# Weight block sums taken from fewer early tiles, Wo's second sums one group later, another final output taken ahead, and butterfly sums made by accumulating DMAs

## Chip, cores and metric

One core of one Trainium2 chip (trn2). The metric is device microseconds of one execution of the whole program. The engines are TensorE (PE in the profile; PEld is its weight load), VectorE (DVE), ScalarE (ACT), GpSimd (POOL) and SyncE (SP); SP, ACT and POOL issue the DMAs.

## What is computed

Eight chunks of 512 tokens with 512 features are normalised, go through a linear attention and through a gated feed-forward part whose weights are meant in a Walsh-Hadamard basis, and the product of both is added to the input:

```
xn = layernorm(x)
k, v, q = xn @ W{k,v,q}.T + b                      # elu(k)+1, elu(q)+1
context = phi_q * cumsum(phi_k * v) * SCALE
s = context @ Wo.T + bo
y = fwht(xn * SU_ug) / 64
h = silu(y @ W_gate.T * ws_gate) * (y @ W_up.T * ws_up)
g = silu(fwht(h * SU_dp) / 64 @ W_down.T * ws_down)
out = x + s * g
```

D is 512, the hidden size of the feed-forward part 2048. The transforms are taken on the weights, once, and not on the tokens.

## The kernel before

**Precision and products.** Each f32 operand is split in a high and a low f16 part, and a product takes three f16 matmuls of 128x512 per pair of operands. Chunks are worked in four pairs. Pair 0 uses plain 2x2 block products, 12 matmuls for a tile. Pairs 1 to 3 use Winograd's form of Strassen's algorithm: seven products (P1 to P7) for four blocks, whose left factors are, besides three plain blocks, four block sums S1 to S4 of the weights, and whose right factors are sums T1 to T4 of the tokens.

**Pieces and groups.** The weights of K, V, Q (two pieces each), of gate and up (eight each, alternating) and of Wo (two, numbers 22 and 23) make 24 pieces, and a group `g` is the work with piece `g`. In pair 0, tile `4 * g + j` is the j-th output block of group `g`; it is also the clock of the preparatory work, which `first_weights` (DVE) and `first_group` (ACT) hang behind certain tiles.

**Butterflies.** Gate's and up's weights of a block `i` (0 to 7) arrive as one load into `raw_ug`. `fly_rows(i, level)` on DVE makes two levels of sums and differences over four rows: level 0 adds and subtracts neighbours from `raw` into `mid`, level 1 from `mid` back into `raw`; each is one addition and one subtraction of 128x1024 f32. `mid` is `fly` (in `x_res`) for `i >= 2`. Level 1 counts `flown` up. ACT and DVE then split the result, PE folds the last levels in, and the piece is stored to DRAM (`scr_g`) and, unsplit, to `scr_f`. `fly_down_level` and `take_down` do the like for the down weights, for which PE's `fold_down` waits.

**Block sums.** For each piece `n` a pass runs over four engines: POOL loads the raw piece (`load_blocks`, for Wo `load_o_blocks`), DVE makes S1 to S4 (`s_sums`, four instructions of 128x256), ACT writes the high half (`s_high`), DVE the low half (`s_low`), POOL stores (`store_sums`). A pass's load waits for the sums of the pass before, its `s_high` for the store before. `S_TILES` lists the tiles of pair 0 behind which DVE makes the sums of passes 0, 1, ...; the next `S_RING - S_EARLY` passes are written out by hand in the stretch at the end of pair 0, and the remaining ones (`late_sums`) hang behind groups of pair 1. `S_RING` is 12 before and after. The first five loads of pair 1's pieces wait for the stores of all 12 (`s_stored`).

**Order of the work.** Each engine's program is one fixed list with semaphore waits; nothing is scheduled at run time. POOL's list alternates loads and stores of the passes with loads for statistics (`load_stats`), reductions over partitions and the accumulating DMAs that add x to an output (`add_tokens`). `STATS_AT` names the groups of pair 1 behind which DVE takes statistics of the next pair's chunks.

**The last outputs.** In pair 3 DVE multiplies gate and attention output (`gated`); POOL then adds x by an accumulating DMA and SP stores, except for the last `LAST_BY_DVE` outputs, where x is loaded beforehand (`load_last_res`) and DVE adds it. For the very last, `last_ahead` multiplies and adds what is known, ACT scales the gate (`scaled_gate`), and `last_output` adds the last product straight from its bank. SP stores the eight outputs strictly in order.

Of the kernel before, what the change touches and what calls it, by code (L numbers as in the profile page):

```python
# [109 lines left out]
OUTS_BEHIND = (8, 11)  # L110
LAST_BY_DVE = 3
# [20 lines left out]
STATS_AT, LATER_STATS_AT = (18, 20), (8, 10)  # L132
# [22 lines left out]
EARLY_STORES = (3, 5)  # L155

# [123 lines left out]
def build(nc, x, x_t, wk_t, wv_t, wq_t, wo_t, ug_t, down_t, vecs, ident_in, hada_in, signs_in, out):  # L280
# [7 lines left out]
    with ExitStack() as ctx_stack:  # L288
# [82 lines left out]
        scaled_gate = work[:, 0, :]  # L371
# [51 lines left out]
        s_late_stored = [sem(f"s_late_stored{s}") for s in range(2)]  # L423
        o_stored, s_o_loaded = sem("o_stored"), sem("s_o_loaded")
# [459 lines left out]
        def _(pool):  # L884
# [39 lines left out]

            def add_tokens(p, n):
# [42 lines left out]
            for n in range(KB):  # L968
                down_bound(n)
            for n in range(PIECES):  # L970
# [40 lines left out]
        def _(act):  # L1011
# [327 lines left out]

            def seven_and_o(p):  # L1340
# [16 lines left out]
                if p == PAIRS - 1:  # L1357
                    c, t = tile_at(p, 2 * TB - 1)
                    act.wait_ge(gate_ready, 8 * p + 8)
                    act.wait_ge(out_scaled, p + 1)  # L1360
                    act.activation(scaled_gate, gate_of(c, t), ACT.Copy, scale=o_out[:, 0:1]).then_inc(gate_scaled, 1)
# [67 lines left out]
            s_high(S_EARLY + 1)  # L1429
            silu_outs(0)  # L1430
            take_out(0)
            s_high(S_EARLY + 2)
            x_high(1, 0)
            t_high(1, 0)
            s_high(S_EARLY + 3)
            x_high(1, 1)
            t_high(1, 1)
            s_high(S_EARLY + 4)
# [27 lines left out]
        def _(dve):  # L1466
# [561 lines left out]
            def last_ahead(p):  # L2028

                c, t = tile_at(p, 2 * TB - 1)  # L2030
                dve.wait_ge(copied, 3 * nth(p, GROUPS + 1) + 2)
                dve.wait_ge(gate_ready, 8 * p + 8)
# [4 lines left out]
            def last_output(p):  # L2037

                c, t = tile_at(p, 2 * TB - 1)
# [656 lines left out]
```

## Time and profile before

| | |
|---|---|
| time, median of 3 runs | 1297.45 us (1297.43 to 1297.5) |
| the profiled execution's own time | 1299.55 us |
| span of the profiled execution | 1297.7 us |
| PE busy | 1260.4 us, 97% |
| DVE busy | 940.5 us, 72% |
| ACT busy | 617.0 us, 48% |
| POOL busy | 100.1 us, 8% |
| DMA: moved, mean | 220.97 MB, 170 GB/s |
| granted TensorE clock, mean | 0.998 |

The span is the time from the first to the last event of the core in the profile; the profiled execution took 2.1 us more than the median of the runs. Matmuls are pipelined and overlap, so that a matmul's mean of 379 ns is not the distance of two. Times in the rows below are us from the span's start unless marked ns, and L numbers are lines of the kernel before.

### The profile page before, as it was taken

What the parts mean: (1) busy time and instruction counts of PE and PEld (TensorE: products, weight loads), DVE (VectorE), ACT (ScalarE), POOL (GpSimd) and SP (SyncE); (2) the same over time, 40 slices, a digit from 0 to 9 for tenths busy, and PEclk for the clock granted to TensorE, in tenths of its full rate; (3) what the DMA queues carried; (4) which work ended last, traced back from release to release, by engine and by line L of the source; (5) the groups of instructions that cost most, each with busy time, mean ns of one, the idle gap of its engine ahead of it and who ended that gap; (6) DMA issues with size and microseconds to landing.
All of it is one profiled execution on the core that took longest, in us unless ns stands there. A gap on an engine that the chain in (4) does not pass through costs nothing.

```text
span 1297.7 us, 16157 instructions
## 1 busy us (share of the span) xinstructions
PE 1260.4 (97%) x5896; PEld 569.9 (44%) x5896; DVE 940.5 (72%) x1420; ACT 617.0 (48%) x911; POOL 100.1 (8%) x150
## 2 busy tenths in 40 slices
PE   5999999999999999989999999999999999999997
PEld 3543444444444444434444444444444444444443
DVE  6989999978746777867882778776773767775714
ACT  5894565631335655543343555554233655554212
POOL 1001001111110000210022001000001000000001
PEclk9999999999999999999999999999999999999999
DMA  9533463777765256565377424323526433232424
GB/s 365 225 130 122 170 225 124 260 245 266 230 229 183 106 197 234 219 217 213 136 218 240 158 107 153 125 103 99 204 96 194 146 114 122 106 130 74 130 89 106
DMA packets 62112, 220.97 MB, mean 170 GB/s; under 512 B 7248, under 2 KB 15184, under 8 KB 47440
## 3 DMA queue, kind: packets, MB, share of 16 engines
q1 hardware_dynamic: 41696, 170.37, 36.2%
q0 software_dynamic: 13056, 37.49, 9.9%
q10 hardware_dynamic: 7280, 12.06, 2.6%
q8 instruction: 47, 0.77, 0.2%
q14 instruction: 33, 0.27, 0.1%
HBM read 166.40 MB, written 53.50 MB: 169 GB/s over the span
## 4 chain that ended last, share of the span: by engine, by line
PE 75%; DVE 11%; ACT 5%; issue 5%; DMA 3%; POOL 0%; SPq 0%; DVEq 0%; ACTq 0%
PE bank L2409 39%; PE bank L2595 13%; PE bank L2289 11%; PE bank L2475 7%; PE bank L2500 2%; PE bank L2620 2%; ACT work L1212 1%; ACT work L1215 1%; DMA h_all<-scr_f 1%; DVE work L1653 1%; PE bank L2334 1%; PE bank L2520 1%; DVE work L1637 1%; DVE work L1680 1%; DVE work L1643 1%
## 5 line engine op out<-in xcount | busy, mean ns | idle before, releaser
L2409 PE MATMUL bank<-xops,ring 128*128 128x512 f16 x2772 | 604.8, 380 | 10.2 <-DVE work L1680 5.5
L2409 PEld LDWEIGHTS bank<-xops,ring 128*128 128x128 f16 x2772 | 269.6, 98 | 344.5 <-issue 16.2
L2289 PE MATMUL bank<-xops,ring 128*128 128x512 f16 x1008 | 225.2, 379 | 0.8 <-DVE ring L1809 0.8
L1195 ACT ACTIVATE work<-bank 128x512 f32<-128x512 f32 x198 | 117.7, 595 | 216.7 <-PE bank L2409 202.2
L1637 DVE TENSOR_TENSOR work<-bank,work 128x512 f32<-128x512 f32 x198 | 133.5, 686 | 115.1 <-PE bank L2409 102.8
L2595 PE MATMUL bank<-h_all,ring 128*128 128x512 f16 x768 | 166.7, 379 | 0.2 <-DVE work L1637 0.2
L2289 PEld LDWEIGHTS bank<-xops,ring 128*128 128x128 f16 x1008 | 98.0, 98 | 124.2 <-issue 8.6
L2595 PEld LDWEIGHTS bank<-h_all,ring 128*128 128x128 f16 x768 | 75.1, 98 | 91.0 <-DVE work L1637 0.7
L1242 ACT ACTIVATE h_all<-work 128x512 f16<-128x512 f32 x116 | 70.3, 624 | 63.3 <-DVE work L1680 63.2
L1689 DVE TENSOR_TENSOR h_all<-work,h_all 128x512 f16<-128x512 f32 x116 | 79.3, 686 | 6.1 <-ACT h_all L1242 4.7
L1643 DVE SCALAR_TENSOR_TENSOR work<-work 128x512 f32<-128x512 f32 x64 | 44.1, 689 | 51.0 <-ACT work L1215 50.7
L2475 PE MATMUL bank<-h_all,ring 128*128 128x512 f16 x288 | 63.5, 379 | 0.0
L1225 ACT ACTIVATE work<-bank,gate_out 128x512 f32<-128x512 f32 x56 | 38.0, 682 | 44.2 <-PE bank L2289 39.8
L1225 ACT ACTIVATE work<-work,gate_out 128x512 f32<-128x512 f32 x72 | 50.8, 714 | 11.7 <-DVE work L1637 11.4
L1680 DVE SCALAR_TENSOR_TENSOR work<-bank,up_out,work 128x512 f32<-128x512 f32 x56 | 41.8, 747 | 17.3 <-issue 7.4
L1680 DVE SCALAR_TENSOR_TENSOR work<-work,up_out 128x512 f32<-128x512 f32 x72 | 52.1, 743 | 0.3
L2475 PEld LDWEIGHTS bank<-h_all,ring 128*128 128x128 f16 x288 | 28.1, 98 | 34.0
L2500 PE MATMUL bank<-h_all,ring 128*128 128x512 f16 x192 | 41.9, 379 | 0.3 <-DVE x_res L2053 0.3
L1658 DVE TENSOR_TENSOR_SCAN work<-work 128x512 f32<-128x512 f32 x32 | 39.2, 1224 | 1.1
L2409 PE MATMUL bank<-ctx,ring 128*128 128x512 f16 x144 | 34.1, 379 | 0.0
L1212 ACT ACTIVATE work<-work,vec,i_attn 128x512 f32<-128x512 f32 x36 | 29.1, 807 | 9.5 <-DVE work L1637 9.5
L2053 DVE TENSOR_TENSOR h_all<-bank,h_all 128x512 f32<-128x512 f32 x8 | 5.4, 689 | 33.4 <-PE bank L2475 29.6
(281 smaller groups left out, 1316.9 us busy)
## 6 DMA issues: line engine op xcount, KB each, us to landing
ring<-scr_g SPq DMA_DIRECT2D x72, 1024.0 KB, 4.8
ring<-scr_d SPq DMA_DIRECT2D x15, 1024.0 KB, 5.7
scr_g<-ring SPq DMA_DIRECT2D x22, 512.0 KB, 3.4
h_all<-in_ug_t SPq DMA_DIRECT2D x8, 1024.0 KB, 13.1
ring<-in_down_t SPq DMA_DIRECT2D x6, 1024.0 KB, 6.5
scr_g<-ring POOLq DMA_DIRECT2D x12, 512.0 KB, 5.0
work<-in_x_t SPq DMA_DIRECT2D x6, 1024.0 KB, 7.0
scr_g<-h_all POOLq DMA_DIRECT2D x12, 512.0 KB, 2.9
```

The lines of the kernel that those rows point to most:

```text
L1195: act.activation(tile(g, j), chain_bank(g)[:, :], ACT.Copy).then_inc(copied, 1)
L1225: act.activation(tile(g, j), src, ACT.Silu, scale=gate_out[:, at:at + 1]).then_inc(act_tiles, 1)
L1242: act.activation(h[:, i, TILE_OF[j], HI, :], tile(g, j), ACT.Copy).then_inc(h_hi, 1)
L1637: dve.tensor_tensor(tile(g, j), at[:, :], tile(g, j), ALU.add).then_inc(summed, 1)
L1643: dve.scalar_tensor_tensor(tile(g, j), exp_tile(n), 1.0, tile(g, j), ALU.min, ALU.add) \
L1680: dve.scalar_tensor_tensor(tile(g, j), src, up_out[:, at:at + 1], tile(g - 1, j), ALU.mult, ALU.mult).then_inc(h_made, 1)
L1689: dve.tensor_tensor(at[:, LO, :], tile(g, j), at[:, HI, :], ALU.subtract).then_inc(h_ready, 1)
L2289: mm = pe.matmul(plain_bank(g, j)[:, :], at[:, s, 2 * dh + kk, r, :], xops[:, kk, xs, PLAIN_B[dh][c], :], start=(n == 0), stop=(n == len(t ...
L2409: mm = pe.matmul(to[:, :], weight_of(slot, s, b, kk), at, start=(a == 0 and m in (P1, P2, P5)), stop=(a == 5), skip_group_check=True)
L2475: mm = pe.matmul(to[:, :], down_weight(slot, d, i, s), at, start=(i == 0 and n == 0 and m in (P1, P2, P5)), stop=(i == SEVEN - 1 and n == ...
L2500: mm = pe.matmul(to[:, :], rest_weight(slot, half, d + 2 * r, i, s), h[:, i, 2 * half + c, xs, :], start=(m == R22 and n == 0), stop=(n == ...
L2595: mm = pe.matmul(d_bank(c, t)[:, :], w[:, t, ws, :], at[:, s, :], start=(a == 0 and b == 0 and n == 0), stop=(a == KB - 1 and b == KB - 1 ...
```

## The change

Four edits:

- **Butterflies of blocks 3 to 7** (`ADDED_FROM = 3`): at level 0 DVE makes only the difference. The sum is made by POOL: a plain DMA of the one set of rows from the input in DRAM into `fly`, a wait for it, and an accumulating DMA of the other set on top (`add_rows`). `add_rows(i)` waits for `flown` to reach `i`, and DVE's level 1 waits for `rows_added`. All ten DMAs stand in POOL's list ahead of the load of pass 1.
- **Block sums**: tiles 27 and 43 leave `S_TILES`. Five passes instead of seven are made behind tiles of pair 0, and seven instead of five by hand after them, in a new order; POOL's reciprocal root for pair 1 (`rstd_of`) moves behind the store of pass 6.
- **Wo's second sums** (piece 23) hang behind group 18 of pair 1 instead of 17, and the first statistics behind group 17 instead of 18.
- **Last outputs**: `LAST_BY_DVE` is 4 instead of 3, and output 4 is treated as the last one: ahead as far as it is known, then finished from its bank. Its x is a fourth load by SP; its accumulating DMA is gone.

```
-OUTS_BEHIND = (8, 11)
-LAST_BY_DVE = 3
+OUTS_BEHIND = (7, 11)
+LAST_BY_DVE, LAST_AHEAD = 4, (4, 7)
-S_TILES = (27, 43, 59, 72, 76, 80, 84)
+S_TILES = (59, 72, 76, 80, 84)
-S_RING = S_EARLY + 5
-S_LATE_FROM, S_LATE_O = 6, {16: GROUPS, 17: GROUPS + 1}
+S_RING = S_EARLY + 7
+S_LATE_FROM, S_LATE_O = 6, {16: GROUPS, 18: GROUPS + 1}
-STATS_AT, LATER_STATS_AT = (18, 20), (8, 10)
+STATS_AT, LATER_STATS_AT = (17, 20), (8, 10)
+ADDED_FROM = 3
...
+            def add_rows(i):
+
+                to = fly.rearrange("p m a b n -> p (m a) b n")[:, :, 0, :]
+                src = ug_t[i, :, :, :, :].rearrange("p m (a b) n -> p m (a b) n", b=2)
+                pool.wait_ge(flown, i)
+                pool.dma_start(to, src[:, :, 0, :]).then_inc(rows_added, 16)
+                pool.wait_ge(rows_added, 32 * (i - ADDED_FROM) + 16)
+                pool.dma_start(to, src[:, :, 1, :], accum_op=ALU.add).then_inc(rows_added, 16)
...
+            for i in range(ADDED_FROM, FP):
+                add_rows(i)
             for n in range(PIECES):
...
                     load_stats(1, 1)
+                if n == S_EARLY + 1:
                     rstd_of(1)
...
+                    if i >= ADDED_FROM:
+                        prep.after(dve.tensor_tensor(to_high, low, high, ALU.subtract))
+                        return
+                else:
+                    if i >= ADDED_FROM:
+                        dve.wait_ge(rows_added, 32 * (i - ADDED_FROM + 1))
...
+            def last_output(p, n):
+
+                c, t = tile_at(p, n)
+                at, m = ((right_bank(GROUPS + 1), P2), (left_bank(GROUPS + 1), P3))[LAST_AHEAD.index(n)]
+                to = 3 * nth(p, GROUPS + 1) + (1, 3)[LAST_AHEAD.index(n)]
+                dve.wait_ge(product_done, products_to(p, GROUPS + 1, m))
+                dve.wait_ge(gate_scaled, LAST_AHEAD.index(n) + 1)
+                dve.tensor_tensor(o_of(c, t), at[:, :], scaled_gate(n), ALU.mult).then_inc(summed, 1)
+                dve.wait_ge(summed, to)
                 dve.tensor_tensor(res_of(c, t), res_of(c, t), o_of(c, t), ALU.add).then_inc(out_ready, 1)
```

The instructions move as follows. PE's list is the same in both kernels.

DVE in pair 1, at the end of group 17 and the start of group 18 (`h_all<-h_all,s_attn` is `s_low` of piece 22, the four 128x256 rows are the sums of piece 23, BN_STATS the statistics, `work<-bank,up_out,work` the use of the block that frees a bank). Before:

```order
L1838 SCALAR_TENSOR_TENSOR h_all<-h_all,s_attn 128x1024
L1828 TENSOR_TENSOR h_all<-h_all 128x256
L1829 TENSOR_TENSOR h_all<-h_all 128x256
L1830 TENSOR_TENSOR h_all<-h_all 128x256
L1831 TENSOR_TENSOR h_all<-h_all 128x256
L1680 SCALAR_TENSOR_TENSOR work<-work,up_out 128x512
L1689 TENSOR_TENSOR h_all<-work,h_all 128x512
L1680 SCALAR_TENSOR_TENSOR work<-bank,up_out,work 128x512
```

DVE in pair 1, the same place in the changed kernel:

```order
L1860 SCALAR_TENSOR_TENSOR h_all<-h_all,s_attn 128x1024
L1540 BN_STATS stats<-x_res 128x6 x2
L1540 BN_STATS stats<-gates 128x6 x2
L1702 SCALAR_TENSOR_TENSOR work<-work,up_out 128x512
L1711 TENSOR_TENSOR h_all<-work,h_all 128x512
L1702 SCALAR_TENSOR_TENSOR work<-bank,up_out,work 128x512
```

The sums of piece 23 now come one group later, where the statistics stood.

DVE at the end of pair 0, from the token sums of pair 1's first half on (`work<-work`: T1 to T4; `xops<-work,xops` 128x1024 and 128x512: low halves of the plain blocks; 128x1024 x2: low halves of T1 to T4; `ring<-ring` 128x256: sums of a pass; `ring<-ring` 128x1024: its low half). Before:

```order
L1606 TENSOR_TENSOR work<-work 128x512
L1611 TENSOR_TENSOR xops<-work,xops 128x1024
L1613 TENSOR_TENSOR xops<-work,xops 128x512
L1828 TENSOR_TENSOR ring<-ring 128x256
L1829 TENSOR_TENSOR ring<-ring 128x256
L1830 TENSOR_TENSOR ring<-ring 128x256
L1831 TENSOR_TENSOR ring<-ring 128x256
L1621 TENSOR_TENSOR xops<-work,xops 128x1024 x2
L1841 TENSOR_TENSOR ring<-ring 128x1024
```

DVE at the end of pair 0, the same place in the changed kernel:

```order
L1628 TENSOR_TENSOR work<-work 128x512
L1850 TENSOR_TENSOR ring<-ring 128x256
L1851 TENSOR_TENSOR ring<-ring 128x256
L1852 TENSOR_TENSOR ring<-ring 128x256
L1853 TENSOR_TENSOR ring<-ring 128x256
L1633 TENSOR_TENSOR xops<-work,xops 128x1024
L1635 TENSOR_TENSOR xops<-work,xops 128x512
L1863 TENSOR_TENSOR ring<-ring 128x1024
L1643 TENSOR_TENSOR xops<-work,xops 128x1024 x2
```

A pass's low half now stands ahead of T's low halves, and with it ACT's `s_high`, which waits for a store, stands ahead of ACT's high half of T.

DVE in the last pair, from output 3 to the add of group 23's C22 (`h_all<-bank,o_out,h_all`: an attention output added up; `h_all<-bank,work`: a product from its bank times the scaled gate). Before:

```order
L2018 TENSOR_TENSOR h_all<-h_all 128x512
L1633 SCALAR_TENSOR_TENSOR h_all<-bank,o_out,h_all 128x512
L2018 TENSOR_TENSOR h_all<-h_all 128x512
L2033 TENSOR_TENSOR h_all<-h_all 128x512
L2035 TENSOR_TENSOR h_all<-h_all 128x512
L1633 SCALAR_TENSOR_TENSOR h_all<-bank,o_out,h_all 128x512
```

DVE in the last pair, the same place in the changed kernel:

```order
L2045 TENSOR_TENSOR h_all<-h_all 128x512
L2071 TENSOR_TENSOR h_all<-bank,work 128x512
L2073 TENSOR_TENSOR h_all<-h_all 128x512
L2060 TENSOR_TENSOR h_all<-h_all 128x512
L2062 TENSOR_TENSOR h_all<-h_all 128x512
L1655 SCALAR_TENSOR_TENSOR h_all<-bank,o_out,h_all 128x512
```

The count is the same here; the two instructions that take output 4 ahead stand earlier, between outputs 1 and 2.

## Rows read from the trace of the kernel before

**Rows 1.** The page: busy time of each engine, share of the span, instructions.

```profile
PE 1260.4 (97%) x5896; PEld 569.9 (44%) x5896; DVE 940.5 (72%) x1420; ACT 617.0 (48%) x911; POOL 100.1 (8%) x150
```

**Rows 2.** Waits of PE: engine, line, releaser: us in total, times, longest.

```profile
PE bank L2409 <- DVE work L1680: 5.5, 5, 3.4
```

**Rows 3.** Timeline of PE, pair 0: start us, us, engine, line, form [idle before].

```profile
114.83 2.76 PE L2289 MATMUL bank<-xops,ring 128*128 128x512 f16 x12 [0.37 <-DVE ring L1809]
...
125.79 1.12 PE L2334 MATMUL bank<-ring,hada 128*128 128x512 f32 x2 [1.30 <-DVE xops L1955]
```

**Rows 4.** Timeline of DVE, the same stretch of pair 0.

```profile
110.70 1.22 DVE L1899 TENSOR_TENSOR h_all<-x_res 128x1024 f32<-128x1024 f32 x1
111.84 0.42 DVE L1828 TENSOR_TENSOR ring<-ring 128x256 f32<-128x256 f32 x1
...
113.43 0.74 DVE L1680 SCALAR_TENSOR_TENSOR work<-bank,up_out,work 128x512 f32<-128x512 f32 x1
...
116.55 1.28 DVE L1838 SCALAR_TENSOR_TENSOR ring<-ring,s_attn 128x1024 f16<-128x1024 f32 x1
...
122.60 1.22 DVE L1899 TENSOR_TENSOR x_res<-h_all 128x1024 f32<-128x1024 f32 x1
...
126.25 1.22 DVE L1898 TENSOR_TENSOR h_all<-x_res 128x1024 f32<-128x1024 f32 x1
```

**Rows 5.** POOL's plain DMAs of 512 KB (L946), from issue to landing.

```profile
DMA to landing us min/median/max: 3.5/3.6/9.0
```

**Rows 6.** POOL's accumulating DMAs of 256 KB (L931), from issue to landing.

```profile
DMA to landing us min/median/max: 3.6/5.9/9.7
```

**Rows 7.** Timeline of DVE in pair 1, around the sums of piece 23.

```profile
555.73 1.28 DVE L1838 SCALAR_TENSOR_TENSOR h_all<-h_all,s_attn 128x1024 f16<-128x1024 f32 x1
560.59 0.42 DVE L1828 TENSOR_TENSOR h_all<-h_all 128x256 f32<-128x256 f32 x1 [3.58 <-DMA h_all<-in_wo_t]
...
562.18 0.74 DVE L1680 SCALAR_TENSOR_TENSOR work<-work,up_out 128x512 f32<-128x512 f32 x1
...
563.45 0.74 DVE L1680 SCALAR_TENSOR_TENSOR work<-bank,up_out,work 128x512 f32<-128x512 f32 x1
...
571.14 1.28 DVE L1518 BATCH_NORM_STATS2 stats<-x_res 128x6 f32<-128x512 f32 x2
```

**Rows 8.** Timeline of PE in pair 1, the same place.

```profile
564.34 30.27 PE L2409 MATMUL bank<-xops,ring 128*128 128x512 f16 x132 [3.44 <-DVE work L1680]
```

**Rows 9.** The stretch behind that wait: us, PE busy (count), granted clock, DMA.

```profile
564.30:567.60 3.30, 3.26 (x8) 0.50 0.04 15
```

**Rows 10.** POOL's loads for the statistics (L906, 540 to 560), to landing.

```profile
DMA to landing us min/median/max: 4.2/4.8/5.4
```

**Rows 11.** Timeline of DVE, end of pair 0.

```profile
322.35 0.43 DVE L1828 TENSOR_TENSOR ring<-ring 128x256 f32<-128x256 f32 x1 [3.36 <-DMA ring<-scr_f]
```

**Rows 12.** Timeline of PE, end of pair 0.

```profile
325.26 4.91 PE L2620 MATMUL bank<-ctx,ring 128*128 128x512 f16 x22
...
387.42 13.11 PE L2409 MATMUL bank<-xops,ring 128*128 128x512 f16 x60
```

**Rows 13.** Timeline of POOL, end of pair 0: the store of pass 11.

```profile
368.43 0.54 POOL L957 DMA_DIRECT2D scr_g<-ring  x1 [8.96 <-DVE ring L1841]
```

**Rows 14.** Stores of passes 9, 10 and 11 (L957, 345 to 372), issue to landing.

```profile
DMA to landing us min/median/max: 3.0/6.8/6.8
```

**Rows 15.** SP's loads of pieces (L774, 360 to 420), issue to landing.

```profile
DMA to landing us min/median/max: 4.7/5.8/8.9
```

**Rows 16.** SP's stores of the last outputs (L806): issue ns, first and last start.

```profile
L806 SPq DMA_DIRECT2D out<-h_all x8: 332/344/453, 1280.3 to 1294.5; - x8
```

**Rows 17.** The same stores, the three issued from 1293.2 to 1294.1, to landing.

```profile
DMA to landing us min/median/max: 2.1/2.4/2.7
```

**Rows 18.** POOL's accumulating DMA for output 4, issued at 1287.5, to landing.

```profile
DMA to landing us min/median/max: 5.7/5.7/5.7
```

**Rows 19.** Timeline of DVE, its last instruction.

```profile
1292.59 0.69 DVE L2043 TENSOR_TENSOR h_all<-h_all 128x512 f32<-128x512 f32 x1
```

More of the change, by code:

```diff
@@ L369, in gate_of, with scaled_gate @@
             return h_tile(t, c % 2)
-        scaled_gate = work[:, 0, :]
+        def scaled_gate(n):
+            return work[:, LAST_AHEAD.index(n), :]
         def ct_sum(p, n):
@@ L1338, in seven_gate, with scale_gate @@
                 act.activation(down_tile(d, j), src, ACT.Silu, scale=d_out[:, t:t + 1]).then_inc(gate_ready, 1)
+            def scale_gate(p, n):
+                act.wait_ge(gate_ready, 8 * p + GATE_ORDER.index(OUT_ORDER[n]) + 1)
+                act.wait_ge(out_scaled, p + 1)
+                act.activation(scaled_gate(n), gate_of(*tile_at(p, n)), ACT.Copy, scale=o_out[:, 0:1]).then_inc(gate_scaled, 1)
             def seven_and_o(p):
@@ L1356, in seven_and_o @@
                     seven_gate(p, d, j)
[L1357 to L1361, printed above, removed]
+                    if p == PAIRS - 1 and OUT_ORDER.index((d, j)) in LAST_AHEAD:
+                        scale_gate(p, OUT_ORDER.index((d, j)))
                 o_groups(p)
@@ L1429, in _ @@
             s_high(S_EARLY + 1)
+            s_high(S_EARLY + 2)
             silu_outs(0)
             take_out(0)
-            s_high(S_EARLY + 2)
+            s_high(S_EARLY + 3)
             x_high(1, 0)
+            s_high(S_EARLY + 4)
             t_high(1, 0)
-            s_high(S_EARLY + 3)
+            s_high(S_EARLY + 5)
             x_high(1, 1)
             t_high(1, 1)
-            s_high(S_EARLY + 4)
+            s_high(S_EARLY + 6)
             silu_outs(1)
@@ L2026, in pair_outputs, with last_ahead @@
                     gated(*tile_at(p, n))
[L2028 to L2032, printed above, removed]
+            def last_ahead(p, n):
+                c, t = tile_at(p, n)
+                dve.wait_ge(copied, 3 * nth(p, GROUPS + 1) + 1 + LAST_AHEAD.index(n))
+                dve.wait_ge(gate_ready, 8 * p + GATE_ORDER.index(OUT_ORDER[n]) + 1)
                 prep.after(dve.tensor_tensor(o_of(c, t), gate_of(c, t), o_of(c, t), ALU.mult))
@@ L2165, in seven_and_o @@
                 add(p, GROUPS, C22)
-                pair_outputs(p, (1, 2))
+                pair_outputs(p, (1,))
+                if p == PAIRS - 1:
+                    last_ahead(p, 4)
+                pair_outputs(p, (2,))
                 add(p, GROUPS, C12)
                 pair_outputs(p, (3,))
-                add(p, GROUPS + 1, C11)
-                pair_outputs(p, (4,))
                 if p == PAIRS - 1:
-                    last_ahead(p)
+                    last_output(p, 4)
+                    last_ahead(p, 7)
+                else:
+                    add(p, GROUPS + 1, C11)
+                    pair_outputs(p, (4,))
                 add(p, GROUPS + 1, C22)
@@ L2176, in seven_and_o @@
                     pair_outputs(p, (6,))
-                    last_output(p)
+                    last_output(p, 7)
                 else:
@@ L2223, in _ @@
                 split_ctx(0, n)
+            s_sums(S_EARLY + 1)
             o_low()
             chunk_stats(1, 1)
+            s_low(S_EARLY + 1)
             for n in range(4, 8):
                 split_ctx(0, n)
-            s_sums(S_EARLY + 1)
+            s_sums(S_EARLY + 2)
             means_and_roots(1)
             out_scale()
-            s_low(S_EARLY + 1)
+            s_low(S_EARLY + 2)
             outputs(0)
-            s_sums(S_EARLY + 2)
+            s_sums(S_EARLY + 3)
             normalise_pair(1)
-            s_low(S_EARLY + 2)
-            x_sums(1, 0)
-            s_sums(S_EARLY + 3)
-            t_low(1, 0)
-            s_low(S_EARLY + 3)
-            x_sums(1, 1)
-            s_sums(S_EARLY + 4)
+            s_low(S_EARLY + 3)
+            x_adds(1, 0)
+            s_sums(S_EARLY + 4)
+            x_low(1, 0)
+            s_low(S_EARLY + 4)
+            t_low(1, 0)
+            s_sums(S_EARLY + 5)
+            x_adds(1, 1)
+            s_low(S_EARLY + 5)
+            x_low(1, 1)
+            s_sums(S_EARLY + 6)
             t_low(1, 1)
-            s_low(S_EARLY + 4)
+            s_low(S_EARLY + 6)
             outputs(1)
```

8 lines of the change are left out of this document (3 added, 5 removed).

## The prediction

> **What bounds the kernel now.** I read the page's busy times first: PE is busy 97% of the span [rows 1], and the change leaves PE's list as it is. So the kernel can only gain where PE stands idle, and at its ends. The second view is the list of PE's waits: the longest single one at work is 3.4 us behind DVE's L1680 [rows 2]. The third is PE's timeline, searched for starts later than the end before. Between the first matmul and the last it has some 30 gaps that sum to 15.4 us. Three lie where the change moves work: 0.37 us at 114.8, 1.30 us at 125.8 [rows 3] and 3.44 us at 564.3 [rows 8]. From 126 to 387 PE does not wait at all, though DVE is nearly full in the first half of that. The fourth view is the tail: DVE's last instruction starts at 1292.6 [rows 19], but SP issues the last store only at 1294.5 [rows 16], more than a microsecond after that output was ready.
>
> **Part 1: early DVE work.** Before 126 PE waits for DVE's backlog. DVE ran from 111.84 to 113.43 on the sums behind tile 27, so 1.6 us, and 1.2 us on their low half at 116.55; the level-0 sum of block 3 takes 1.1 us, the step between its addition and its subtraction, which started at 122.60 [rows 4]. The change removes all three ahead of the instruction PE waits for at 125.8. Ahead of the wait at 114.8 only the first 1.6 us goes. Both waits are smaller than what goes ahead of them (0.37 against 1.6; 1.30 against 3.9), and a wait can't give back more than itself: **gain 0.37 + 1.30 = 1.7 us**. The lower bound is 0, if other work has become due at the same time. The same removal at tile 43 and for blocks 4 to 7 is worth nothing: PE has no wait there, it is slack for DVE.
>
> What is added is a wait. Level 1 of block 3 needs both DMAs. They can start when `flown` reaches 3, at 111.9, the end of L1899 at 110.70, and DVE gets to level 1 at about 126.25 − 3.9 = 122.4 [rows 4]. The trace has no accumulating DMA of 512 KB. The nearest rows are a plain one of 512 KB by POOL, 3.6 us median (3.5 to 9.0) [rows 5], and an accumulating one of 256 KB, 5.9 us median (3.6 to 9.7) [rows 6]. One behind the other that is 9.5 us in the middle, and the second is twice as large here, so I take 11 us: rows at 123, half a microsecond of DVE waiting. The ends are 7.1 us (119.0, no wait) and 18.7 us (130.6). PE was served in time with level 1 starting at 126.25, and everything behind it is lighter now, so lateness up to there costs nothing and the far end at most 130.6 − 126.25 = 4.4 us. Queued behind DVE's wait are uses of blocks that free PE's banks. For blocks 4 to 7 eight tiles, over 20 us, lie between one level 1 and the next: hidden. POOL's list puts all ten DMAs ahead of the load of pass 1, so that load can't go before block 6 is flown, about 205; its sums are due some 40 us later: hidden too.
>
> The Trainium skill (DMA: Bandwidth & Descriptors, "Anatomy of one DMA — SWDGE (gpsimd) path") gives a DMA from GpSimd 2.0 us plus its bytes at 436 GB/s, an estimate of 3.2 us for each of the two, and the rows would be in at 118.3 with no wait. The trace agrees for the best plain DMA (3.5 us) and not for accumulating ones, whose median is 5.9 us for half the bytes; by the page the sum below is the same and the rival of late rows loses its chance, by the rows it keeps one.
>
> **Part 2: two passes more at the end of pair 0.** Each costs DVE 1.6 + 1.2 us. The first fits where DVE idled 3.36 us before 322.35 [rows 11]; the splits of the context, done at 319.0, then end near 322, and PE reads them at 325.3 [rows 12]. From the outputs of chunk 0 on, four passes stand where three did. There each pass waits for the store before it, and those took 6.8, 6.8 and 3.0 us [rows 14]. Walking the new list with these: low half of pass 9 at 357.5, T's low halves end at 361.6 (ACT's part now stands behind a store), sums 10 and the next token sums to 366, low half 10 at 368, plain low halves and sums 11 at 372, T at 374.3, low half 11 at 377.3 with a store of 6.8 us before it. The last store is then issued at 377.4 instead of 368.4 [rows 13], lands 3.0 us later, and SP's first load of a pair-1 piece 4.7 us after that [rows 15]: 385.1. PE wants it at 387.4 [rows 12]. The tokens are ready at 374.3. **Cost 0**, covered by PE's work on pair 0, with 2.3 us of cover left. What is late next is that first load, and without cover it costs PE its lateness one for one.
>
> **Part 3: Wo's second sums.** At 557 DVE stood 3.58 us waiting for Wo's rows [rows 7]; behind it hung L1680 at 563.45, which frees PE's bank, and PE idled 3.44 us [rows 8]. Then PE's granted clock stood at 0.50 of full, 1.2 GHz, for 3.3 us [rows 9], so the work of 1.65 us took 3.3. The wait costs 3.44 + 1.65 = 5.1 us. With the change statistics stand there: two rows of 1.28 us, about 2.4 us together [rows 7]. Their loads were issued from 549 to 551, took 4.8 us, at most 5.4 [rows 10], and are in by 556. DVE: low half from 555.73, 1.2 us; statistics 2.4; then L1680, L1689, L1680, which took from 562.18 to 564.19, 2.0 us. Sum 561.3, and 0.15 us to the first matmul: 561.5. PE ran dry at 564.34 − 3.44 = 560.9. A gap of 0.6 us stays, at full clock as behind the 1.3 us gap. **Gain 5.1 − 0.6 = 4.5 us** (bounds 0 and 5.1). Piece 23's rows landed at 560.6 and its sums now come near 565, at the end of an even group, where PE had no wait: nothing. Statistics' second loads go out earlier, beside a weight load that has over 25 us: nothing.
>
> **Part 4: the tail.** Output 4's accumulating DMA was issued at 1287.5 and took 5.7 us [rows 18], to 1293.2; SP's stores are in order, so the four last left between 1293.2 and 1294.5 [rows 16] and the last took the longest of the four. Now output 4 is ready near 1287, and store 7 waits for DVE alone: 1293.3, 1.2 us earlier. The first of the four took 2.1 us, the others more, up to 2.7 [rows 17]; alone, the last should take 2.1. **Gain 1.2 + 0.6 = 1.8 us** (bounds 1.2 and 1.9). DVE's chain from output 3 on has the same number of instructions. The two taken ahead fall between outputs 1 and 2, where DVE waits for ACT; they may push output 2 by some tenths, and its store isn't the last. The extra load of x goes with the three that were there, long ahead of its use, and ACT's scaling of another gate falls in its idle time.
>
> **Sum.** 1.7 + 4.5 + 1.8 = 8.0 us. Against the profiled execution's own 1299.55 us that gives 1291.6; that execution stands 2.1 us above the median of the runs, and I take the difference off the median: 1297.45 − 8.0 = **1289.5 us**.
>
> **Rivals.**
> - *Statistics take the place of the wait.* If their loads, or group 18's own work, hold DVE as Wo's rows did, the 4.5 us stay: 1294.0. Against: these loads are issued ahead of Wo's by POOL, and took 4.8 us [rows 10]. Chance 0.10.
> - *The early gaps don't go.* Either they hang on work the change does not move (then 1289.5 + 1.7 = 1291.2; the change would not do there what it takes DVE work away for), or the rows of block 3 land late, up to 1289.5 + 4.4 = 1293.9, more likely near 1291. For: the wide spread of the accumulating DMAs [rows 6]. Chance 0.12.
> - *PE waits at the start of pair 1.* The place is 387.4, the mechanism the chain of stores and high halves of Part 2. With the long ends of the rows, 9.0 for 6.8 us twice (the first hop is in both lists), 9.0 for the last store's 3.0 and 8.9 for the load's 4.7, the piece comes 2.2 + 2.2 + 6.0 + 4.2 = 14.6 us later than forecast, 12.3 us after PE wants it; with the slow clock behind such a wait, 1.65 us as in Part 3, 1289.5 + 14.0 = 1303.5, slower. It decides against the change from a chain that is 2.3 + (8.0 − 1.65) = 8.7 us later than forecast. Against: three of four long ends at once, while the DMA queues there move nothing else for POOL. Chance of slower than before 0.04, of a small wait (to 1292.5) 0.06.
>
> **How the numbers follow.** The forecast has 0.68, with its own range 1288.8 (no gap left in Part 3, 1.9 in the tail, 1297.45 − 8.7) to 1290.6. The rest is the rivals' 0.10, 0.12 and 0.10. About 0.2%, 2.6 us, is what a measurement of this kernel can tell. Faster by more, under 1294.85, holds the forecast, the first rival, most of the second and the small wait: 0.91. Within 0.2%: 0.05, the ends of several cases together. Slower: 0.04. The range goes from 1288.4 to 1293.0, which leaves out the first rival and the far ends.
>
> **What would show it.** Right: PE's timeline has no gap at 114.8 and 125.8, a gap under 1 us at about 559.5 with the granted clock at 1.00 behind it, none near 386; the last store is issued right behind DVE's last instruction. Rows of block 3 are seen in a wait of L1925, level 1, near 122, under a microsecond or two. Wrong: a wait of DVE for a DMA above 4 us at either place, a matmul that waits for a load of `scr_g` at pair 1's start, or a store of output 3 that holds up the last four.

## The result

| | kernel before | changed kernel |
|---|---|---|
| time, median | 1297.47 us (1297.43 to 1297.67) | 1291.17 us (1290.05 to 1291.18) |
| ratio | | 0.9949 [0.9932, 0.9966] |
| profiled execution, span | 1299.55, 1297.7 us | 1291.18, 1289.4 us |

Four executions of each. The time fell by 6.3 us, 0.5%, where 8.0 was forecast. 1291.17 lies in the stated range of 1288.4 to 1293.0, but outside the 1288.8 to 1290.6 that the prediction gave its forecast without the rivals. The two profiled executions are 8.3 us of span apart.

### The profile page after: what moved, and what is told of

It reads as the page before. It is cut to its first block, busy times and chain, and to the rows that moved or that the text cites. A ratio compares the mean times of both kernels' runs of the same rounds, so it can differ in the third digit from the quotient of the medians.

```text
span 1289.4 us, 16166 instructions
## 1 busy us (share of the span) xinstructions
PE 1259.5 (98%) x5896; PEld 570.7 (44%) x5896; DVE 936.1 (73%) x1417; ACT 618.3 (48%) x912; POOL 108.9 (8%) x159
## 4 chain that ended last, share of the span: by engine, by line
PE 78%; DVE 9%; issue 5%; ACT 5%; DMA 3%; SPq 0%; DVEq 0%; ACTq 0%
PE bank L2450 40%; PE bank L2636 13%; PE bank L2330 12%; PE bank L2516 7%; PE bank L2541 2%; PE bank L2661 2%; ACT work L1229 1%; ACT work L1232 1%; DMA h_all<-scr_f 1%; DVE work L1675 1%; PE bank L2375 1%; PE bank L2561 1%; DVE work L1659 1%; DVE work L1665 1%; DVE work L1702 1%
## 5 line engine op out<-in xcount | busy, mean ns | idle before, releaser
L2450 PE MATMUL bank<-xops,ring 128*128 128x512 f16 x2772 | 603.2, 379 | 7.4 <-DVE work L1702 2.6
L2450 PEld LDWEIGHTS bank<-xops,ring 128*128 128x128 f16 x2772 | 269.4, 98 | 340.2 <-issue 11.1
L1702 DVE SCALAR_TENSOR_TENSOR work<-bank,up_out,work 128x512 f32<-128x512 f32 x56 | 41.8, 747 | 22.0 <-issue 14.7
L1702 DVE SCALAR_TENSOR_TENSOR work<-work,up_out 128x512 f32<-128x512 f32 x72 | 52.2, 743 | 0.3
L1680 DVE TENSOR_TENSOR_SCAN work<-work 128x512 f32<-128x512 f32 x32 | 39.2, 1224 | 1.1
L2450 PE MATMUL bank<-ctx,ring 128*128 128x512 f16 x144 | 34.0, 379 | 0.0
```

The lines of the kernel that those rows point to most:

```text
L1702: dve.scalar_tensor_tensor(tile(g, j), src, up_out[:, at:at + 1], tile(g - 1, j), ALU.mult, ALU.mult).then_inc(h_made, 1)
L2450: mm = pe.matmul(to[:, :], weight_of(slot, s, b, kk), at, start=(a == 0 and m in (P1, P2, P5)), stop=(a == 5), skip_group_check=True)
```

## The profile after

The page, busy times and instructions, as [rows 1]:

```profile
PE 1259.5 (98%) x5896; PEld 570.7 (44%) x5896; DVE 936.1 (73%) x1417; ACT 618.3 (48%) x912; POOL 108.9 (8%) x159
```

PE has the same 5896 matmuls in a span 8.3 us shorter. Its gaps sum to 10.0 us where it was 15.4; 0.9 of the difference is a gap at 20 us that costs nothing, since PE stands 0.4 us behind the changed kernel both ahead of it and after it. The waits of PE, as [rows 2] (L1680 is now L1702, L2409 is L2450):

```profile
PE bank L2450 <- DVE work L1702: 2.6, 5, 0.8
```

The longest is 0.8 us, no longer 3.4. **Early pair 0**: PE's timeline where 0.37 and 1.30 us stood [rows 3].

```profile
106.50 1.13 PE L2375 MATMUL bank<-ring,hada 128*128 128x512 f32 x2 [1.08 <-DVE ring L1958]
...
113.93 2.75 PE L2330 MATMUL bank<-xops,ring 128*128 128x512 f16 x12
...
123.42 1.02 PE L2375 MATMUL bank<-ring,hada 128*128 128x512 f32 x2
124.28 5.34 PE L2330 MATMUL bank<-xops,ring 128*128 128x512 f16 x24
```

No bracket stands at 113.93 or 123.42: both waits are gone, and none follows until pair 1. A gap of 1.08 us ahead of them, which the change does not touch, stays. DVE and POOL in the same stretch (L1918 is the lone subtraction of level 0, L1925 level 1; L935 the plain and L937 the accumulating DMA):

```profile
118.30 1.22 DVE L1918 TENSOR_TENSOR x_res<-h_all 128x1024 f32<-128x1024 f32 x1
...
124.49 1.23 DVE L1925 TENSOR_TENSOR h_all<-x_res 128x1024 f32<-128x1024 f32 x1 [2.45 <-DMA x_res<-in_ug_t]
```

```profile
111.85 0.78 POOL L935 DMA_DIRECT2D x_res<-in_ug_t  x1 [26.16 <-DVE h_all L1926]
117.19 1.24 POOL L937 DMA_DIRECT2D x_res<-in_ug_t  x1 [4.56 <-DMA x_res<-in_ug_t]
```

The plain DMA started when the forecast had it, landed 5 us later and the second 7.3 us after its issue. DVE waits 2.45 us, where half a microsecond was forecast.

**End of pair 0**, POOL's last store, SP's first loads of pieces, and PE:

```profile
374.15 0.54 POOL L971 DMA_DIRECT2D scr_g<-ring  x1 [6.53 <-DVE ring L1863]
```

```profile
377.07 8.65 SPq L779 DMA_DIRECT2D ring<-scr_g  x5
```

```profile
385.20 13.11 PE L2450 MATMUL bank<-xops,ring 128*128 128x512 f16 x60
```

PE starts pair 1 without a wait, 2.2 us earlier than in [rows 12]. The last store left at 374.2, where 377.4 was forecast, and the piece PE wants was in.

**Pair 1.** DVE, then PE, at the place of [rows 7] and [rows 8], and the granted clock behind it, as [rows 9]:

```profile
553.49 1.28 DVE L1860 SCALAR_TENSOR_TENSOR h_all<-h_all,s_attn 128x1024 f16<-128x1024 f32 x1
554.68 1.28 DVE L1540 BATCH_NORM_STATS2 stats<-x_res 128x6 f32<-128x512 f32 x2
555.88 1.27 DVE L1540 BATCH_NORM_STATS2 stats<-gates 128x6 f32<-128x512 f32 x2
```

```profile
559.21 28.65 PE L2450 MATMUL bank<-xops,ring 128*128 128x512 f16 x132 [0.55 <-DVE work L1702]
```

```profile
559.15:562.45 3.30, 3.24 (x16) 1.00 0.96 309
```

The statistics' rows were in. The gap is 0.55 us, the clock stays at 2.4 GHz, and the 132 matmuls take 28.65 us instead of 30.27.

**The tail.** SP's stores (the last of the seven issued from 1278.8 on), and DVE's last instruction, as [rows 16, 19]:

```profile
1285.89 0.69 DVE L2073 TENSOR_TENSOR h_all<-h_all 128x512 f32<-128x512 f32 x1
```

```profile
L811 SPq DMA_DIRECT2D out<-h_all x1: 332/332/332, 1286.6 to 1286.6; - x1
...
DMA to landing us min/median/max: 2.3/2.3/2.3
```

The last store leaves at 1286.61, right behind DVE's end at 1286.58. From PE's last matmul to the end of the span it is 5.4 us; before it was 7.0.

**Not forecast.** POOL's list between two stores:

```profile
313.64 0.54 POOL L971 DMA_DIRECT2D scr_g<-ring  x1 [6.25 <-DVE ring L1863]
323.53 1.68 POOL L895 TENSOR_TENSOR rstd<-var_eps,minus_half 128x8 f32<-128x8 f32 x1 [9.35 <-issue]
```

```profile
325.25 0.17 DVE L1583 TENSOR_SCALAR mean_root<-mean_var 128x8 f32<-128x8 f32 x1 [5.20 <-POOL rstd L895]
```

POOL's root (`rstd`) starts 9.35 us after the store ahead of it has been issued. The bracket names "issue", so the profile shows nothing that it waits for, and DVE waits 5.20 us for it. Before, the root stood at 313.99 behind a wait of 11.41 us for DVE. PE has no gap here in either kernel.

## Experiments

Theory, called A below: each term of the sum is a wait that ends with DVE or with one store, and goes by as much as the work ahead of it goes. The rivals are named with each run. The runs were made in three sets of four, each set on one chip and beside its own executions of the kernel before, on a chip that was another one in each set: 16 in the first set (median 1298.3), 16 in the second (1297.81), 21 in the third (1298.6). A distance between runs of two sets is therefore given against each set's own kernel before as well, where it matters.

### The first set: where the two microseconds are

The two microseconds are those between the forecast 8.0 and the measured 6.3.

**e1** is the kernel before, unchanged.

> The kernel before, once more, to see an execution other than the profiled one. Its profiled execution took 1299.55 us and its timed ones 1297.47. Theory A: the 2.1 us of difference lie in the wait for Wo's rows in pair 1 (a landing that scatters), so that a profile of an execution of 1297.5 us shows PE's gap before L2409 near 563 as 1 to 2.5 us, with the granted clock at or near 1.00 behind it, instead of 3.44 us and 0.50. Theory B: they lie elsewhere (start, end, other landings); the gap is again 3.3 to 3.6 us with the slow clock behind it, whatever the time.

1298.58 us (1297.62 to 1300.4, 10 executions), ratio 1.0003 [0.9994, 1.0012]; span 1296.0. PE at Wo's sums, and the stretch behind:

```profile
563.02 1.28 PE L2409 MATMUL bank<-xops,ring 128*128 128x512 f16 x5 [3.27 <-DVE work L1680]
```

```profile
563.10:566.40 3.30, 3.30 (x11) 0.65 0.00 0
566.40:569.70 3.30, 3.30 (x15) 0.83 0.03 5
```

The wait for Wo's rows is there again, 3.27 us, with a slow clock behind it in both rows (0.65 and 0.83 of full). That is theory B. Between this profile and the one before lie 1.7 us of span: 0.6 at the start, 0.4 between (0.7 less in waits from 486 to 564, 0.3 more later), 0.7 behind PE's last matmul (6.3 us against 7.0). So the kernel's own executions scatter, from 1295.4 to 1301.3 over the three sets, and the profiled execution that the prediction was read from stood high by no single cause.

**e2** is the kernel before with Part 3 alone.

```
-S_LATE_FROM, S_LATE_O = 6, {16: GROUPS, 17: GROUPS + 1}
+S_LATE_FROM, S_LATE_O = 6, {16: GROUPS, 18: GROUPS + 1}
-STATS_AT, LATER_STATS_AT = (18, 20), (8, 10)
+STATS_AT, LATER_STATS_AT = (17, 20), (8, 10)
```

> The kernel before with Part 3 of the change alone. PE's gap near 561 becomes 0.5 to 0.7 us at full clock. Theory A: 1295.0 us (2.4 less than 1297.47, since the usual execution loses only that much more to the wait). Theory B: 1293.0 us (4.5 less), and what the whole change lacks is given back by another part.

1294.71 us (1293.24 to 1295.77), ratio 0.9973 [0.9962, 0.9984]: 3.6 us under the kernel before, between theory A's 2.4 and theory B's 4.5. PE's gap at 561.8 is 0.55 us; against the profile before, PE stands where it stood up to there (a wait ends at 524.10 and 524.08), and 4.15 us earlier from 590 on. The two early gaps are unchanged, 0.37 and 1.30 us.

**e3** is the changed kernel without Part 4 (output 4 by POOL's DMA as before).

```
-LAST_BY_DVE, LAST_AHEAD = 4, (4, 7)
+LAST_BY_DVE, LAST_AHEAD = 3, (4, 7)
...
-                if p == PAIRS - 1:
-                    last_ahead(p, 4)
...
-                    last_output(p, 4)
```

> The changed kernel with output 4 again added by POOL's accumulating DMA: three outputs by DVE, one ahead. If Part 4 is worth 1.7 us as forecast: 1292.9 us, the last four stores leave within about 1.3 us of each other behind the landing of output 4's DMA, the last at least 1 us behind DVE's last instruction. Rival: the last store's landing is what ends the program either way, and the time stays within 0.5 us of 1291.2.

1291.75 us (1290.72 to 1292.08), ratio 0.9948 [0.9931, 0.9965]; PE ends at 1284.2, beside 1284.0 in the changed kernel, and 6.1 us pass from there to the end, against 5.4. The last store is issued 0.3 us behind DVE's end and lands in 2.7 us. The forecast 1.7 us are not there: the time is 0.6 us above the changed kernel's, but the distance to its own set's kernel before, 6.6 us, is that of e8, and the store is not held up by 1 us. The rival's limit was 0.5.

**e4** is the changed kernel without accumulating DMAs: DVE makes all of level 0 again.

```
-ADDED_FROM = 3
+ADDED_FROM = 8
```

> The changed kernel with all of level 0 on DVE again (no accumulating DMAs), block sums as changed. Theory: the removal of the sums behind tile 27 alone (2.8 us of DVE ahead of the 1.3 us wait) clears both early gaps, and the DMAs are worth nothing: 1291.2 us, no gap of PE between 107 and 385, DVE's step at L1925 of block 3 without a wait. Rival: without the DMAs DVE stays behind and PE waits near 124 again, 0.3 to 1.2 us slower.

1291.77 us (1290.89 to 1292.05), ratio 0.995 [0.9935, 0.9964], 6.5 us under the kernel before, and PE within 0.2 us of the changed kernel all the way. DVE at level 1 of block 3:

```profile
119.54 1.22 DVE L1926 TENSOR_TENSOR x_res<-h_all 128x1024 f32<-128x1024 f32 x1
...
123.20 1.22 DVE L1925 TENSOR_TENSOR h_all<-x_res 128x1024 f32<-128x1024 f32 x1
```

No gap from 107 to 398. The addition costs DVE 1.1 us and saves it the wait of 2.45: level 1 starts at 123.20 instead of 124.49. **With tile 27 free, the accumulating DMAs of this change give nothing.**

### The second set: one place each

**e8** is the changed kernel again, beside the next three.

> The changed kernel itself, unchanged, for a second comparison on the same chip as the next three. Theory A (the 6.3 us of the first comparison and the 8.3 us between the two profiled executions differ only by the scatter of the kernel before, whose executions spread over 1295.4 to 1300.4): this kernel's own executions stay within about 1.2 us of each other, at 1290 to 1291.5, and the difference from the kernel before lies between 6 and 8. Theory B (the profiled execution before showed the true cost, 8.3 us): the difference is above 7.5 again.

1291.17 us (1290.81 to 1293.13), ratio 0.9949 [0.9937, 0.9961], 6.6 us under the kernel before; span 1289.3. DVE's wait at level 1 is 2.37 us. Median and ratio repeat, and the difference lies where theory A has it; theory B's 7.5 doesn't come. One execution, 1293.13, lies above theory A's 1291.5.

**e5** sums rows by DMA from block 2 on. The two waits added for block 2 are those that DVE's level 0 has there.

```
-ADDED_FROM = 3
+ADDED_FROM = 2
...
                 pool.wait_ge(flown, i)
+                if i == 2:
+                    pool.wait_ge(piece_made, QKV_GROUPS)
+                    pool.wait_ge(d_squared, KB)
```

> Blocks are summed by accumulating DMAs from block 2 on instead of 3, so DVE drops one more level-0 sum of 1.1 us ahead of the wait at 106.5. Theory A (the 1.08 us gap there is DVE's backlog, as the two gaps that went were): the gap falls by up to 1.08, time 0.5 to 1.1 us under the changed kernel. Theory B (rows of an accumulating pair come 12 us after the block is flown, and at block 2 nothing covers them): DVE waits 2 to 5 us at level 1 of block 2, PE's gap grows by that less the slack, time 1 to 4 us above the changed kernel.

1290.47 us (1289.12 to 1291.5), ratio 0.994 [0.9927, 0.9952]. POOL, and PE where 1.08 us stood:

```profile
86.24 0.78 POOL L938 DMA_DIRECT2D x_res<-in_ug_t  x1
90.56 1.24 POOL L940 DMA_DIRECT2D x_res<-in_ug_t  x1 [3.55 <-DMA x_res<-in_ug_t]
```

```profile
106.04 1.13 PE L2378 MATMUL bank<-ring,hada 128*128 128x512 f32 x2
```

The gap is gone. Block 2's rows are in long before DVE asks for them, since it asks at 108.8, 22 us after the first DMA's issue; for block 3 it asks after 10. Here an accumulating pair pays: it takes 1.1 us off DVE ahead of a wait of 1.08, as theory A has it. The gap is seen to go; the time alone, 0.7 us under e8 with overlapping intervals, does not show it.

**e6** puts POOL's root one store earlier, behind DVE's result that it needs.

```
-                if n == S_EARLY + 1:
+                if n == S_EARLY:
                     rstd_of(1)
```

> POOL's rstd of the second row of late tokens stands one store earlier, where POOL waits for DVE anyway. Theory A (the 9.4 us ahead of rstd are the reload of POOL's code, which runs as soon as its instruction is reached): the wait of 5.2 us that DVE shows ahead of L1583 at 325 goes or falls under 1 us, the spread load isn't waited for at 338.5, PE has no gap in either kernel there, time within 0.3 us of the changed kernel. Theory B (the 9.4 us belong to the store ahead of it): they move with the store and DVE's wait stays.

1290.78 us (1290.46 to 1291.39), ratio 0.9944 [0.9933, 0.9956]. POOL:

```profile
313.31 2.78 POOL L895 TENSOR_TENSOR rstd<-var_eps,minus_half 128x8 f32<-128x8 f32 x1 [12.42 <-DVE var_eps L1550]
```

The root follows DVE at once and the 5.20 us are gone (DVE now waits 2.15 us for a pass's load). The delay goes where the root goes and does not show where POOL waits anyway. It is not a fixed time. e8 is the changed kernel too, and there it is shorter:

```profile
325.64 1.68 POOL L895 TENSOR_TENSOR rstd<-var_eps,minus_half 128x8 f32<-128x8 f32 x1 [6.82 <-issue]
```

In the seven profiles in which the root stands right behind the store it is 9.35 (the changed kernel), 6.99 (e3), 7.32 (e4), 7.80 (e5), 7.21 (e7), 6.82 (e8) and 8.69 us (e10), and in each the root starts 2.2 to 3.6 us after that store has landed. So two readings are open, and no run separates them: POOL changes its code for this instruction, or the root waits until the store ahead has landed. In e6 the store ahead of it, issued at 300.35, had landed 7.1 us later, long before the root's turn, so e6 fits both. It isn't every instruction that waits for a store: in the changed kernel a reduction starts at 284.90 while the store of 281.51, which took 7.6 us to land, is under way. PE, with no gap there before, gains nothing, as theory A had it.

**e7** is the changed kernel without Part 3, the reverse of e2's edit.

```
-S_LATE_FROM, S_LATE_O = 6, {16: GROUPS, 18: GROUPS + 1}
+S_LATE_FROM, S_LATE_O = 6, {16: GROUPS, 17: GROUPS + 1}
-STATS_AT, LATER_STATS_AT = (17, 20), (8, 10)
+STATS_AT, LATER_STATS_AT = (18, 20), (8, 10)
```

> The changed kernel with Wo's second sums and the statistics back at their groups of before (17 and 18). Theory A (the 4.5 us of Part 3 are the wait for Wo's rows and the slow clock behind it): PE's gap near 561 is 3.3 to 3.5 us again, the granted clock behind it 0.50 for 3.3 us, time 3.5 to 5 us above the changed kernel (e2, Part 3 alone, moved 3.6 to 4.2). Theory B (once the early parts are gone the wait is shorter, since DVE is further ahead): the gap is the same or longer, since an engine that is further ahead waits longer for rows that come at a time of their own; under 2 us would speak against A.

1294.44 us (1292.12 to 1299.59, 11 executions), ratio 0.9978 [0.9967, 0.999]: 3.3 us above e8. DVE, PE and the clock:

```profile
558.34 0.42 DVE L1850 TENSOR_TENSOR h_all<-h_all 128x256 f32<-128x256 f32 x1 [2.91 <-DMA h_all<-in_wo_t]
```

```profile
562.09 1.24 PE L2450 MATMUL bank<-xops,ring 128*128 128x512 f16 x5 [2.77 <-DVE work L1702]
```

```profile
562.10:565.40 3.30, 3.30 (x11) 0.70 0.02 10
565.40:568.70 3.30, 3.30 (x13) 0.78 0.02 5
```

The same two losses, PE's gap a little under what was expected: 2.77 us, while 3.27 and 3.44 stood in the two profiles of the kernel before. How late Wo's rows are differs from execution to execution, and so does the clock. The slow stretch takes 0.0013 off an execution's mean granted clock (0.30 and 0.22 over 3.3 us each), and four of the eleven executions have a mean of 1.000 and so no such stretch. They took 1292.1 to 1294.4 us, the seven others, at 0.997 to 0.999, 1294.1 to 1299.6. By 698 PE is 4.6 us behind e8 in the profile, 2.9 of it at this wait and 1.7 in the slow stretch; in the median it is 3.3.

### The third set: the edges

**e9** joins e5 and e6.

> Blocks summed by accumulating DMAs from block 2 on (e5) and POOL's rstd one store earlier (e6), together. Theory A (e5's 0.7 us under the changed kernel are the 1.1 us gap at 106.5 that went, e6 moves no time): 1290.0 to 1290.7, no PE gap from 90 to 397, DVE's 5.2 us wait at 325 gone. Theory B (e5's median was the scatter between executions): the median is back at 1291.2, though the gap stays away.

1289.23 us (1288.61 to 1291.13), ratio 0.9932 [0.9919, 0.9945]: the lowest median of all, 9.4 us under the kernel before. PE has no gap from 90 to 397. The profiled execution is the slowest of its five (1291.13, span 1289.3, the span of e8): PE starts 0.3 us later there, waits at 521 and 540 are longer than e8's by 0.9 us together, and by 559 nothing of the 1.1 us is left (559.19, in e8 559.15). The intervals of e9 and of the changed kernel in e8 overlap by a little, so that it beats the kernel before is shown, and that it beats the changed kernel by the 1.1 us of the gap is likely, not shown by times alone.

**e10** issues block 3's plain DMA twice, one behind the other.

```
                 pool.wait_ge(flown, i)
+                if i == 3:
+                    pool.dma_start(to, src[:, :, 0, :]).then_inc(rows_first, 16)
+                    pool.wait_ge(rows_first, 16)
                 pool.dma_start(to, src[:, :, 0, :]).then_inc(rows_added, 16)
```

> The changed kernel with the plain DMA of block 3's rows issued twice, the second behind the first one's landing, so that the sums come about 5 us later and nothing else moves: DVE's wait at level 1 of block 3 grows from 2.4 to some 7.5 us and level 1 starts near 129.5. Theory A (lateness costs nothing up to a start at 126.25 and one for one behind it): PE gets a gap of up to 3.3 us behind 126, time 2 to 3.3 us above the changed kernel. Theory B (DVE has slack behind the wait as well, since the two sums of tile 27 and their low half are gone too): PE's gap stays under 1 us. With the slow clock behind a long gap the cost could be 1.6 us more than the gap.

1295.74 us (1293.76 to 1296.63, 11 executions), ratio 0.9977 [0.9968, 0.9986], 4.6 us above e8, or 3.8 if each is taken against its own set's kernel before. DVE, and two of PE's four new waits:

```profile
129.00 1.23 DVE L1929 TENSOR_TENSOR h_all<-x_res 128x1024 f32<-128x1024 f32 x1 [6.91 <-DMA x_res<-in_ug_t]
```

```profile
151.65 2.76 PE L2334 MATMUL bank<-xops,ring 128*128 128x512 f16 x12 [0.83 <-DVE ring L1835]
...
156.37 1.12 PE L2379 MATMUL bank<-ring,hada 128*128 128x512 f32 x2 [1.53 <-DVE ring L1962]
```

Level 1 comes 4.5 us later than in the changed kernel. PE has no gap at 126, and four, of 0.48, 0.46, 0.83 and 1.53 us, between 143 and 157; it starts pair 1's second stretch at 402.43 instead of e8's 398.67, 3.8 us later. DVE is so full after block 3 that it carries the debt for 15 to 28 us and then hands it to PE nearly whole: from level 1 on to 156 it idles 2.0 us in e8 and 1.5 here. Both theories are wrong on the place, and A on the amount: the free lateness is some 0.7 us (4.5 less 3.8), not 1.8.

**e11** is e9 without Part 4 (e3's edit).

> e9 without Part 4, so that the fourth output ahead is compared on the same chip. Theory A (forecast of Part 4): 1.2 to 1.9 us above e9. Theory B (the 1.2 us were one late landing of output 4's accumulating DMA in the profiled execution before, as e1's tail, 6.3 us from PE's end to the span's against 7.0, suggests): 0.3 to 0.9 us above e9, the last store issued within 0.7 us of DVE's last instruction, its landing not shorter in e9 by more than 0.3.

1291.29 us (1291.08 to 1293.09), ratio 0.9948 [0.9935, 0.996]: 2.1 us above e9 in the median, more than either theory had, and 0.7 in the span of the profiled executions (1290.0 and 1289.3), as theory B. The last store leaves 0.5 us behind DVE's end. From PE's last matmul to the end of the span:

| output 4 by POOL's DMA | before 7.0, e2 6.4, e1 6.3, e11 6.2, e3 6.1 |
|---|---|
| output 4 ahead | e4 6.1, e8 5.6, changed kernel 5.4, e9 5.4, e10 5.4, e7 5.3, e12 5.2, e5 5.1, e6 5.1 |

The means are 6.4 and 5.4: Part 4 is worth 1.0 us in the profiles, while medians leave it between nothing (e3) and 2.1 us (e11). Output 4's accumulating DMA took 5.7 us to land in the profile before and 5.0, 5.1, 4.7 and 4.9 in e1, e2, e3 and e11. One profile with it, e4, has 6.1: there output 3's accumulating DMA landed 5.5 us after its issue at 1279.45, not 4.8, the stores queued behind it, and the last took 2.9 us to land.

**e12** puts the first pass back behind tile 27 and keeps the accumulating DMAs.

```
-S_TILES = (59, 72, 76, 80, 84)
+S_TILES = (27, 59, 72, 76, 80, 84)
-S_RING = S_EARLY + 7
+S_RING = S_EARLY + 6
```

One pass fewer stands in the lists at the end of pair 0.

> The changed kernel with the first pass of block sums back behind tile 27 (and one pass fewer at the end of pair 0), the accumulating DMAs kept. Theory A (both early gaps are DVE's backlog, and what goes ahead of each pays for it): PE's gap at 114.8 is back with about 0.3 us, the one at 125.8 with little (1.30 less the 1.1 of block 3's level-0 sum, plus what the wait for the rows adds, 0 to 1.5 us), time 0.3 to 2 us above the changed kernel. Theory B (the wait for block 3's rows sits in slack that DVE only has because tile 27's 2.8 us are gone): the wait shrinks to nothing here, since DVE comes 2.8 us later. At the end of pair 0 one pass fewer gives nothing, PE starts pair 1 at the same distance.

1300.1 us (1299.24 to 1302.13, 11 executions), ratio 1.0012 [1.0003, 1.0021]. PE early on:

```profile
114.67 2.76 PE L2327 MATMUL bank<-xops,ring 128*128 128x512 f16 x12 [0.37 <-DVE ring L1830]
...
124.49 1.13 PE L2372 MATMUL bank<-ring,hada 128*128 128x512 f32 x2 [0.16 <-DVE xops L1981]
```

The first gap is back to the hundredth, and of the second 0.16 us are left: 1.30 less the 1.14 of the level-0 addition. Theory A's numbers, and DVE doesn't wait for the rows, as B says. But the kernel is 8.9 us slower than e8 (8.1 if each is taken against its own set's kernel before), which no theory had. POOL's load, DVE and PE near 211, and the clock behind:

```profile
207.44 3.27 POOL L956 DMA_DIRECT2D ring<-in_wv_t  x4
```

```profile
214.46 0.43 DVE L1849 TENSOR_TENSOR ring<-ring 128x256 f32<-128x256 f32 x1 [10.57 <-DMA ring<-in_wv_t]
```

```profile
217.46 3.17 PE L2327 MATMUL bank<-xops,ring 128*128 128x512 f16 x7 [5.54 <-DVE ring L1830]
```

```profile
217.40:220.70 3.30, 3.24 (x8) 0.50 0.79 288
```

Pass 1 now stands at tile 59, and POOL's list has its load behind all ten DMAs of the butterflies, so it goes out at 207.4, 3.5 us after DVE was free for it, and DVE loses 10.57 us until it has landed. PE loses 5.54 us in the gap and 1.65 at half speed; with the two early gaps that is 7.7 us. The changed kernel has its pass 0 at that tile, whose load stands ahead of the ten. So with the DMAs in this place of POOL's list two passes have to leave, not one, since they block the list until block 6 is flown.

## Why the prediction was right

- **The sum.** 8.0 was read from one profiled execution and taken off the median. Against that execution it holds: 8.3 us of span, 0.4 of it from a start that no part of the change touches. In the medians of its two comparisons the change is worth 6.3 and 6.6. The step that failed is this transfer: two of the three terms contain landing times of DMAs, and the one execution had long ones. That 1291.17 lies in the range all the same is in part luck: the forecast's own values end at 1290.6, and the room above them was there for late rows and a wait at pair 1's start, neither of which cost PE anything.
- **Part 1, 1.7 us.** Between [rows 12] and the profile after, PE's start of pair 1 moves up by 2.2 us, of which 0.36 lie ahead of 88 us: 1.86, 0.2 more than the two waits. Both waits went; e12 brings back the first, with 0.37. Of the second it has 0.16, which is 1.30 less the 1.14 of the addition that stays away: a wait can't give back more than itself, and it goes by what goes ahead of it. What the part credits to the accumulating DMAs was not needed (e4).
- **The rows of block 3.** The pair took 5.0 and 7.3 us, 12.6 with POOL's issue in between, where 11 was taken from [rows 5, 6]. With DVE free at 122.0 (forecast 122.4) the wait was 2.45 us, not 0.5. It cost PE nothing, but for less margin than the text claims: "lateness up to there costs nothing" took 126.25 from the kernel before, while PE itself moves up by some 2.2 us with the change. In the changed kernel's own time that limit is about 124.0, and level 1 at 124.49 was already past it (e10 leaves some 0.7 us more). e10 also shows the price behind: 3.8 us of PE for 4.5 us of lateness, the rival's mechanism, later than its place. The Trainium skill (DMA: Bandwidth & Descriptors, "Anatomy of one DMA — SWDGE (gpsimd) path") would have had the rows in at 118.3, an estimate of 3.2 us for each DMA; the trace has 5.0 and 7.3, and the measurement decides.
- **Part 2, 0 us.** No wait at pair 1's start. The chain of stores was 3.3 us shorter than walked and PE was there 2.2 us earlier, so the cover was some 3.4 us instead of 2.3. What was forgotten is POOL's root, moved behind a store, and the delay ahead of it of 9.35 us (6.8 to 9.35 in seven profiles), whose cause stays open. A DVE wait of 5.20 us came of it, 2.67 in e8. It was luck that it cost nothing: PE had its operands.
- **Part 3, 4.5 us.** The two profiles show 4.5: [rows 8] and the rows after are 5.1 us apart, 1.6 more by the end of the 132 matmuls, less the 2.2 from Part 1. The gap left is 0.55 (0.6 forecast) at full clock. In medians it is 3.6 (e2) and 3.3 (e7 against e8): the term was some 1 us too large for a typical execution. Its size came from one execution with the longest of the three gaps seen (3.44, 3.27 and 2.77 us) and with the slow stretch, which four of e7's eleven executions do not have.
- **Part 4, 1.8 us.** The profiles show 1.6 (7.0 to 5.4), the tails of all fourteen profiles 1.0. The step that failed is the landing of output 4's DMA, 5.7 us in [rows 18], which the text took for the rule, where four other profiles have 4.7 to 5.1; in e1 the last store left at 1292.8, 0.5 us behind DVE and not 1.2. The last store's landing fell from 2.7 at most to 2.3, and to 2.0 to 2.9 in other runs, where 2.1 was assumed.
- With 1.7 + 3.4 + 1.0 the sum is 6.1, beside 6.3 and 6.6 measured. So the waits were the right ones, and the terms of Parts 3 and 4 were too large.
- **The rivals.** Statistics did not take the wait's place, the early gaps went, pair 1 started in time. The slow branch's mechanism is real all the same, at another place: e12's late load cost 5.54 us and half speed, and made the kernel slower than before.

## What to carry over

Take a wait's size from several executions when a DMA's landing sets it, and a sum from one profile as the sum for that execution. Count lateness against the engine that is served, whose own time moves with the change, and look for the price of a late operand where the full engine runs out of slack, which was 15 to 28 us on, not where it waits. When DMAs go ahead of others in an engine's list, ask of each one behind them when it can leave now and who needs it first.

## What the runs showed of the hardware

- POOL's root of two tensors had 6.8 to 9.35 us ahead of it that no releaser explains in the seven profiles where it stood right behind a store, and started 2.2 to 3.6 us after that store's landing; with POOL waiting for DVE ahead of it, no such time shows (e6).
- An accumulating DMA of 512 KB from DRAM into SBUF by POOL landed 6.0 to 9.7 us after its issue (median 8.1 of five), a plain one of the same size 4.0 to 5.0 (4.2), in the changed kernel's profile.
- PE's granted clock fell behind waits of 2.77, 3.27, 3.44 and 5.54 us, to 0.50 in a stretch of 3.3 us or to 0.65 to 0.83 in two, and cost 1.6 us (profile before), 1.65 (e12) and 1.7 (e7); it stayed at 1.00 behind those of up to 1.53.
- The kernel before took between 1295.4 and 1300.2 us on one chip, and up to 1301.3 on three; the changed kernel, with its waits for Wo's rows and output 4's DMA gone, 1290.1 to 1293.1 in nine executions. With Wo's wait back (e7) it was 1292.1 to 1299.6.
